# Adapter tail with its second products in high and low parts, and shares spread over partitions out of one SBUF row instead of a DRAM array

## The reference, cut to what matters

```python
# layer 0, after a convolution and causal attention (16 heads)
probs = jax.nn.softmax(tok @ gate_w.T, axis=-1)
topv, topi = jax.lax.top_k(probs, TOP_K)                     # 2 of 8 experts
topw = topv / (jnp.sum(topv, axis=-1, keepdims=True) + 1e-09)
combine = jnp.zeros((T, E), tok.dtype).at[jnp.arange(T)[:, None], topi].set(topw)
eo = jnp.einsum('eti,edi->etd', jax.nn.silu(eg) * eu, wd)    # inner width 176
moe_out = jnp.einsum('te,etd->td', combine, eo)
# layer 1: modulated attention and a GELU feed-forward, then
probs = jax.nn.softmax(x_flat @ Wr.T + br, axis=-1)
expert_idx, expert_weight = jnp.argmax(probs, axis=-1), jnp.max(probs, axis=-1)
h = jnp.einsum('nd,erd->ner', x_flat, A)                     # 8 adapters of rank 64
y = jnp.einsum('ner,eor->neo', h, B) * SCALING
out = take_along_axis(y, expert_idx) * expert_weight         # added to x
```

## Time and profile before

| what | us |
|---|---|
| median of 3 runs | 627.74 |
| lowest to highest | 626.38 to 632.41 |
| the profiled execution | 626.71 |
| its span in the profile | 624.6 |
| PE busy | 593.3 |
| DVE, ACT, POOL busy | 377.1, 341.1, 209.7 |

### The profile page before, as it was taken

One profiled execution on the slowest core, in us unless ns is written; L12 is line 12 of the kernel. 1 busy time (PEld: TensorE's weight loads), 2 busy tenths in 40 slices (PEclk: granted clock), 3 DMA queues, 4 the chain that ended last, 5 costly groups with the idle time before them and its releaser, 6 DMA issues.

```text
span 624.6 us, 13447 instructions
## 1 busy us (share of the span) xinstructions
PE 593.3 (95%) x5492; PEld 500.1 (80%) x5492; DVE 377.1 (60%) x668; ACT 341.1 (55%) x864; POOL 209.7 (34%) x222
## 2 busy tenths in 40 slices
PE   4789999999999989999998999999999998999996
PEld 2678888888888878888877878888788887788875
DVE  4877778877886567886745253262515376684553
ACT  0778568866785534453446453555444456556440
POOL 0672444354436523552434040131403025432000
PEclk9899999999999999999999999999999999999999
DMA  7770000000000148355001030112110001300023
GB/s 204 273 274 7 2 2 2 3 2 2 1 3 6 59 111 267 119 180 174 2 1 44 26 101 2 34 36 68 47 57 0 2 0 36 84 18 1 0 70 134
DMA packets 13676, 38.35 MB, mean 61 GB/s; under 512 B 2320, under 2 KB 3856, under 8 KB 13008
## 3 DMA queue, kind: packets, MB, share of 16 engines
q1 hardware_dynamic: 13376, 36.46, 17.9%
q10 hardware_dynamic: 240, 1.05, 0.7%
HBM read 36.39 MB, written 1.11 MB: 60 GB/s over the span
## 4 chain that ended last, share of the span: by engine, by line
PE 80%; DVE 8%; ACT 5%; DMA 3%; issue 2%; SPq 1%; POOL 1%; ACTq 0%; DVEq 0%
PE ps L1537 20%; PE ps L1538 18%; PE ps L1539 18%; PE ps L1655 8%; PE ps L1845 4%; PE ps L1614 3%; PE ps L1644 2%; PE ps L1632 2%; PE ps L1833 1%; DVE strm_lo L1369 1%; DMA work<-in_cols 1%; PE ps L2031 1%; ACT strm_hi L932 1%; PE ps L1693 1%; SPq L447 1%
## 5 line engine op out<-in xcount | busy, mean ns | idle before, releaser
L519 POOL TENSOR_TENSOR w_lo<-raw_w,w_hi 128x1024 fp32r<-128x1024 f32 x24 | 58.6, 2460 | 159.1 <-ACT w_hi L666 139.4
L1369 DVE SCALAR_TENSOR_TENSOR strm_lo<-ps,col,strm_hi 128x512 fp32r<-128x512 f32 x32 | 24.0, 750 | 104.3 <-ACT strm_hi L932 103.4
L1537 PE MATMUL ps<-w_hi,act_hi 128*128 128x512 f32 x160 | 64.6, 404 | 3.9 <-ACT junk L659 3.1
L917 ACT ACTIVATE work<-ps,col 128x512 f32<-128x512 f32 x64 | 43.9, 689 | 44.6 <-PE ps L1539 44.6
L1537 PE MATMUL ps<-act_hi,w_hi 128*128 128x512 f32 x160 | 63.5, 397 | 3.1 <-ACT work L917 1.9
L1539 PE MATMUL ps<-w_hi,act_lo 128*128 128x512 f32 x160 | 62.5, 391 | 0.0
L1538 PE MATMUL ps<-w_lo,act_hi 128*128 128x512 f32 x160 | 62.5, 390 | 0.0
L1539 PE MATMUL ps<-act_hi,w_lo 128*128 128x512 f32 x160 | 62.4, 390 | 0.0
L1538 PE MATMUL ps<-act_lo,w_hi 128*128 128x512 f32 x160 | 62.3, 390 | 0.0
L1655 PE MATMUL ps<-raw_w,xT 128*128 128x256 f32 x256 | 61.3, 380 | 0.0
L1655 PEld LDWEIGHTS ps<-raw_w,xT 128*128 128x128 f32 x256 | 46.3, 190 | 5.3
(11 more groups left out here) (202 smaller groups left out, 1435.0 us busy)
## 6 DMA issues: line engine op xcount, KB each, us to landing
raw_w<-in_w_attn SPq DMA_DIRECT2D x20, 512.0 KB, 3.6
raw_s<-in_w_moe SPq DMA_DIRECT2D x11, 384.0 KB, 5.1
work<-comb_dram SPq DMA_DIRECT2D x21, 128.0 KB, 2.9
raw_w<-in_w_qkv SPq DMA_DIRECT2D x4, 512.0 KB, 6.2
raw_w<-in_w_o SPq DMA_DIRECT2D x1, 2048.0 KB, 9.0
work<-comb_dram SPq DMA_DIRECT2D x8, 256.0 KB, 5.2
raw_s<-in_w_ffn SPq DMA_DIRECT2D x8, 256.0 KB, 2.7
bd<-in_w_ada SPq DMA_DIRECT2D x1, 1536.0 KB, 7.1
```

The source lines that it names most:

```text
L519: G.tensor_tensor(flat(w_lo[:, slot]), raw, flat(f32(w_hi[:, slot])), ALU.subtract).then_inc(s_piece_lo, 1)
L917: A(dst[:, h * BANK:(h + 1) * BANK], src, ACT.Identity, bias=c_(b, 4 * j + h)).then_inc(s_q1_copied, 1)
L1369: V.scalar_tensor_tensor(flat(strm_lo[:, n % SS]), ps[:, 4 + n % 2, :], c_("bv", 4 * UNITS[u][0] + h), flat(f32(strm_hi[:, n % SS])), ALU. ...
L1537: mm(dst, ah, bh, start=start and i == 0, stop=False, **flags)
```

## The change

Two things are changed.

The array in DRAM goes. spread reads the row of cmbT or selT in SBUF directly, n times, and SP no longer stores it and waits. The number of spreads, their sizes and their place in SP's order stay:

```diff
-            def spread(dst, layer, m, width, done_sem, s=slice(0, TOK)):
+            def spread(dst, rows, m, width, done_sem, s=slice(0, TOK)):
...
-                    sp.dma_start(dst[at:at + n, :], comb_dram[layer, e:e + 1, s].broadcast_to([n, s.stop - s.start])).then_inc(done_sem, 16)
+                    sp.dma_start(dst[at:at + n, :], rows[e:e + 1, s].unsqueeze(1).broadcast_to([1, n, s.stop - s.start])).then_inc(done_sem, 16)
...
                 sp.wait_ge(s_combT_ready, c + 1)
-                sp.dma_start(comb_dram[0, :, s], cmbT[0:NE, s]).then_inc(st_comb, 16)
-                sp.wait_ge(st_comb, 16 * (c + 1))
                 for m in range(SS):
-                    spread(cb[:, m, s], 0, m, INTER, (ld_cb, ld_cb_second)[c][m], s)
+                    spread(cb[:, m, s], cmbT, m, INTER, (ld_cb, ld_cb_second)[c][m], s)
...
                 sp.wait_ge(s_hm_ready, UNIT[m - SS, CHUNKS - 1] + 1)
-                spread(cb[:, m % SS, :], 0, m, INTER, ld_cb[m % SS])
+                spread(cb[:, m % SS, :], cmbT, m, INTER, ld_cb[m % SS])
...
                 sp.wait_ge(s_selT_ready, c + 1)
-                sp.dma_start(comb_dram[1, :, s], selT[0:NE, s]).then_inc(st_comb, 16)
-                sp.wait_ge(st_comb, 16 * (CHUNKS + c + 1))
                 for n in range(c * MR, (c + 1) * MR):
                     m = LORA[n][0]
-                    spread(cb1[:, m, s], 1, m, RANK, ld_cb1[n], s)
+                    spread(cb1[:, m, s], selT, m, RANK, ld_cb1[n], s)
```

The adapters' second products are made from high and low parts. ACT rounds the weight rows and hmk, POOL and DVE subtract for the low parts, and PE's three matmuls take the place of one in f32. The order of the tail on PE and ACT is changed, and DVE's four additions stand behind all multiplies:

```diff
+            for i, m in enumerate(ROWS):
+                pool.wait_ge(s_rows_hi, i + 1)
+                G.tensor_tensor(rows_lo[:, m, :], rows_of(m), f32(rows_hi[:, m, :]), ALU.subtract).then_inc(s_rows_lo, 1)
...
+                if n >= NF - 3:
+                    act.wait_ge(s_ffn_down, MM + 2)
+                    for m in (ROWS[0:2], ROWS[2:3], ROWS[3:4])[n - NF + 3]:
+                        A(rows_hi[:, m, :], rows_of(m), ACT.Copy).then_inc(s_rows_hi, 1)
+
+            def hmk_hi(n):
+                act.wait_ge(s_hmk32, n + 1)
+                act.wait_ge(s_lora_up, MR)
+                if n >= 2:
+                    act.wait_ge(s_hmk_used, n - 1)
+                A(act_hi[:, n % 2, 0:BANK], hmk[:, n % 3, :], ACT.Copy).then_inc(s_hmk_hi, 1)
+
             router_exp(0)
             take_ups(0, 2)
             x4_hi(1)
-            take_ups(2, MR)
+            take_ups(2, 3)
             take_selT(0)
             router_exp(1)
-            take_ups(MR, NL)
+            take_ups(3, 6)
             take_selT(1)
+            take_ups(6, 7)
+            hmk_hi(0)
+            take_ups(7, NL)
+            for n in range(1, NL):
+                hmk_hi(n)
...
+            def share_lo(n):
+                dve.wait_ge(s_hmk_hi, n + 1)
+                V.tensor_tensor(act_lo[:, n % 2, 0:BANK], hmk[:, n % 3, :], f32(act_hi[:, n % 2, 0:BANK]),
+                                ALU.subtract).then_inc(s_hmk_ready, 1)
+
+            share(0)
+            for n in range(1, NL):
+                share(n)
+                share_lo(n - 1)
+            share_lo(NL - 1)
+            for a in range(TILES // 2):
+                add_lora(a)
...
-                    last = mm(ps[:, bank, (t % 2) * D:(t % 2 + 1) * D], hmk[:, n % 3, t * P:(t + 1) * P], rows,
-                              start=(n % MR == 0 and t % 2 == 0), stop=(n % MR == MR - 1), skip_group_check=True)
+                    own = slice(t * P, (t + 1) * P)
+                    last = split_mm(ps[:, bank, (t % 2) * D:(t % 2 + 1) * D],
+                                    [(act_hi[:, n % 2, own], act_lo[:, n % 2, own], rows_hi[:, m, :], rows_lo[:, m, :])],
+                                    start=(n % MR == 0 and t % 2 == 0), stop=(n % MR == MR - 1), skip_group_check=True)
...
             for n in range(NL):
-                if n == 2:
+                if n == 3:
                     logits1(1)
-                if n == MR:
                     turn_sel(0)
+                if n == 6:
+                    turn_sel(1)
                 lora_up(n)
-            turn_sel(1)
             for n in range(MR):
                 lora_down(n)
```

More of the change, by code:

```diff
@@ L113, in build_program @@
         ps = ctx.enter_context(nc.psum_tensor("ps", [P, 8, BANK], F32))
-        comb_dram = nc.dram_tensor("comb_dram", [2, NE, TOK], F32, kind="Internal").ap()
         def c_(name, k=0, n=1):
@@ L219, in build_program @@
         ld_slice = [sem(f"ld_slice{i}") for i in range(SS)]
-        st_comb = sem("st_comb")
         ld_cb = [sem(f"ld_cb{i}") for i in range(SS)]
@@ L333, in build_program @@
         s_wsel = sem("wsel")
+        s_hmk32 = sem("hmk32")
+        s_hmk_hi = sem("hmk_hi")
         s_hmk_ready = sem("hmk_ready")
+        s_rows_hi = sem("rows_hi")
+        s_rows_lo = sem("rows_lo")
+        s_lora_sum = sem("lora_sum")
         block = ctx.enter_context(nc.Block())
@@ L382, in z2_at, with rows_of @@
             return hid[:, CT + t, :] if t < CT else z2[:, t, :]
+        rows_hi, rows_lo = (w[:, 2].rearrange("p a b -> p (a b)").rearrange("p (m n) -> p m n", m=MR) for w in (w_hi, w_lo))
+        ROWS = (0, MR - 1, 1, 2)
+        def rows_of(m):
+            return raw_t[:, 1, 2 * D:3 * D] if m == MR - 1 else raw_t[:, (MM + m) % SS, D:2 * D]
         LORA = [(m, c) for c in range(CHUNKS) for m in (0, 3, 1, 2)]
@@ L1504, in _, with add_lora, share @@
             router_pick(1)
[L1506 to L1512, removed]
-            for n, (m, c) in enumerate(LORA):
+            def add_lora(a):
+                if a % 2 == 0:
+                    dve.wait_ge(s_lora_sum, a // 2 + 1)
+                else:
+                    dve.wait_ge(s_hmk_used, MR * (a // 2 + 1))
+                t2 = slice(2 * a, 2 * a + 2)
+                V.tensor_tensor(xres[:, t2, :], ps[:, (a + 2) % 4, :].rearrange("p (b n) -> p b n", b=2),
+                                xres[:, t2, :], ALU.add).then_inc(s_y_ready, 1)
+            def share(n):
+                m, c = LORA[n]
                 dve.wait_ge(s_up_copied, n + 1)
@@ L1517, in _ @@
                 if n >= 3:
-                    dve.wait_ge(s_hmk_used, n - 2)
+                    dve.wait_ge(s_hmk_ready, n - 2)
                 V.tensor_tensor(hmk[:, n % 3, :], h1[:, n, :], cb1[:, m, c * BANK:(c + 1) * BANK],
-                                ALU.mult).then_inc(s_hmk_ready, 1)
-                if n == MR + 2:
-                    add_lora(0)
-            add_lora(1)
+                                ALU.mult).then_inc(s_hmk32, 1)
+            def share_lo(n):
[9 more added lines that the diff above has]
+                add_lora(a)
         @block.tensor
@@ L2026, in lora_down @@
                 pe.wait_ge(s_hmk_ready, n + 1)
-                rows = raw_t[:, 1, 2 * D:3 * D] if m == MR - 1 else raw_t[:, (MM + m) % SS, D:2 * D]
+                pe.wait_ge(s_rows_lo, ROWS.index(m) + 1)
                 for t in range(CT):
                     bank = (2 * c + t // 2 + 2) % 4
-                    last = mm(ps[:, bank, (t % 2) * D:(t % 2 + 1) * D], hmk[:, n % 3, t * P:(t + 1) * P], rows,
-                              start=(n % MR == 0 and t % 2 == 0), stop=(n % MR == MR - 1), skip_group_check=True)
+                    own = slice(t * P, (t + 1) * P)
+                    last = split_mm(ps[:, bank, (t % 2) * D:(t % 2 + 1) * D],
+                                    [(act_hi[:, n % 2, own], act_lo[:, n % 2, own], rows_hi[:, m, :], rows_lo[:, m, :])],
+                                    start=(n % MR == 0 and t % 2 == 0), stop=(n % MR == MR - 1), skip_group_check=True)
+                    if n % MR == MR - 1 and t == 1:
+                        last.then_inc(s_lora_sum, 1)
                 last.then_inc(s_hmk_used, 1)
             for n in range(NL):
-                if n == 2:
+                if n == 3:
                     logits1(1)
-                if n == MR:
                     turn_sel(0)
+                if n == 6:
+                    turn_sel(1)
                 lora_up(n)
-            turn_sel(1)
             for n in range(MR):
```

## The result

The changed kernel takes 797.88 us (median of 4 runs, 796.69 to 799.87) against 628.62 for the one before beside it (626.38 to 632.41): a ratio of 1.267, interval 1.261 to 1.273. The forecast was 834, with a range of 695 to 888. The direction and the cause were right; the loss is 169 us and not 207.

A forecast was written before the change was run, and what follows sets the result against it. PE was taken to bound the kernel, except for a last 25 us chained through DRAM round trips. The profiled 626.7 us plus 147 (expert stage) and 60 (tail) gave 833.7, forecast as 834 us, range 695 to 888.

The forecast's parts named there:

- The price, 27.3 GB/s for a block: All spreads: reading one SBUF row gets the rate of one block of four adjacent partitions, 27.3 GB/s.
- Rival A: All spreads: one-row reads go as fast as from DRAM, SP's issue stays the limit; 624 us, chance 0.20.
- rival B: All spreads: the source as a whole is limited to 51 GB/s; 699 us, chance 0.08 including speeds towards the forecast.
- C: All spreads: one DMA engine moves all, 26 GB/s, engines' share one sixteenth; chance within the forecast's 0.72.
- Step 1: Expert stage: shares read from one SBUF row land late, last at 439.5, and DVE's multiply waits; +147 us.
- 5.90 MB at 421 GB/s, 14.0 us: Expert stage: expert slices and attention pieces between the spreads in the first-in-first-out queue add 14.0 us.
- All engines wait behind DVE's multiply: Expert stage: nothing of the next stage can go ahead of DVE's multiply in the engines' orders.
- The 2 us for PE's clock: After the expert stage's wait: 2 us lost as PE's clock is granted at 0.74 when it runs again.
- Step 2: Adapter products: 96 matmuls of 256 columns replace 32 in f32, 11.5 us, 2.8 us gained on PE if fed.
- Step 3: Tail order: earlier turns and no store let the first spread go out at 597.8, 3.4 us earlier.
- Step 4: Tail transfers: adapter spreads from one SBUF row land late, end at 684.4 against 624.6; +60 us.
- 2.10 MB at 27.3 GB/s: Tail: the adapters' 16 spreads at one block's rate take 76.8 us.

The follow-up runs named there:

- e1: Changed kernel with the DRAM array, its stores and waits put back, split adapter products and new order kept; 629.17 us, ratio 0.999.
- e4: Changed kernel with each expert's row of shares on 16 partitions (e, e+8, ...), spreads reading 16 SBUF rows, not one; 626.67 us, ratio 0.995.
- e5: e4 with four places, not two, for the adapters' high and low parts, and chunk 0's additions before the last subtraction; 625.71 us, ratio 0.995.
- e3: Changed kernel with the tail's spreads issued tile 0, 1, 3, 2 in place of 0, 3, 1, 2; 809.04 us, ratio 1.285.
- e8: Kernel before with sixteen-row spreads out of SBUF and no DRAM array, its own tail with f32 adapter products kept; 630.54 us, ratio 1.001.

## Why the prediction came out as it did

**The price, 27.3 GB/s for a block: right.** It was taken from a row at full share and few partitions. The first half tiles run at 27.2, and the last four tiles, all in one block, land from 349.37 to 426.88: 2.10 MB in 77.5 us, 27.1. Rival A is out (e1 and e4 show what it would have been), rival B is out (27, not 51), and so is C: the share is 0.88 to 0.92, not 0.06.

**Step 1, +147, measured +131.9.** Of these, 2.2 us lie ahead of everything that the change touches: the first copy of shares starts at 214.59, before at 212.43. With that taken off, the last share, forecast for 439.5 and used at 426.96, came 14.7 us early. The term that failed is "5.90 MB at 421 GB/s, 14.0 us". The stage took about as long as if these loads were free: the first spread was issued at 215.18, and 0.75 us to the first byte and 5.77 MB at 27.3 make 427.2. But that this fits so well is partly luck, for the landings show a cost that stayed and a gain that I hadn't priced:

- The loads are free only in part. Four attention pieces stand behind the last half tile (landed 274.74); tile 3 landed at 297.44, 22.7 us later, where its 524 KB alone need 19.3. So these loads cost 3.4 us of the 5.0 I gave them. Between the spreads of the last four tiles stand 2.62 MB of loads, 6.2 us at 421 GB/s, and those 77.5 us are what the spreads alone need (77.1 at 27.2).
- Tiles 5 and 6 took 32.4 us and not 38.5 (317.01 to 349.37). There the spreads pass from experts 0 to 3 to experts 4 to 7, and two blocks are read side by side.

The stretch of 320 to 336 us, 60 GB/s at a share of 0.85, holds both: tile 5 from two blocks, and the slice that landed at 334.31. That engines which are done with their part of a spread go on to the load behind it, while the others still wait for the block, is my reading; no experiment tests it.

"All engines wait behind DVE's multiply" was wrong in part, too. DVE waited 77.6 us for shares and not over 100, and for part of the stage it was the expert weights that were late. Both stand in one queue, so the stage's length is the queue's all the same. The rest of the step held: 3 us of catching up were 3.4 (the last four multiplies take 9.13 us, before 12.54). The 2 us for PE's clock didn't come: from the last multiply to the last addition it took 288.9 us, before 288.75. Inside the stage and the tail the clock did fall, and matmuls took longer (the down products' first ones 366 ns in the mean, before 314), so PE counts 627.2 us busy and not the forecast 590.

**Step 2, PE's 2.8 us.** Right as a size, as e5 shows (11.8 us in place of 14.3), and right that waits would eat it here. It isn't free with quick transfers either: e1 gives it back to the round through ACT and DVE. Case A's sum, 2.7 us under before, is near e4, which is that case: 2.05 us by the tails.

**Step 3, 3.4 us earlier.** The first spread is issued 4.42 us after the last addition, before 8.15: 3.7.

**Step 4, +60, measured +38.7.** The term that failed is 2.10 MB at 27.3 GB/s. They took 55 us, from 730.2 (first bytes) to 785.2, 38 GB/s. LORA's order of tiles is 0, 3, 1, 2: experts 0 and 1, then 6 and 7, then 2 and 3, then 4 and 5. Neighbours in the queue lie in different blocks and run beside each other in part. I had priced each tile by one block and not asked what the next one reads. e3 took that away and lost 11 us.

So both misses have one root: I added up the transfers as if each had the queue to itself. Reads of different blocks run side by side in part, and loads to all partitions add little time of their own. The queue does hold back when they land, as the expert weights show.

## What to carry to other kernels

Before moving the source of a broadcast from DRAM to SBUF, count two things: how many limits of 27 GB/s the source's partitions reach (a block of four partitions and the one 32 on are one), and how many engines its outer dimension allows. Then ask what else stands in the same queue: it lands behind the slow transfer, and whoever needs it waits as well. Replicate the row by the engine that makes it (e8, with sixteen copies, is no slower than the kernel before) rather than reading one partition many times. An edit that shortens PE's work in a tail pays only when the transfers ahead and the buffers behind it are eased with it.

## What the runs showed of the hardware that I had not expected

A DMA issue can block the issuing engine. The spreads' line on SP, first before the change and then after it (ns for one issue: least, median, most; then us to landing):

```profile
L447 SPq DMA_DIRECT2D work<-comb_dram x44: 309/546/601, 214.5 to 612.9; - x44
...
DMA to landing us min/median/max: 2.5/3.0/9.8
```

```profile
L455 SPq DMA_DIRECT2D work<-work x44: 478/2140/18228, 215.2 to 773.2; - x44
...
DMA to landing us min/median/max: 7.0/15.0/55.9
```

One issue took 18.2 us, and the sixteen of the tail 48: SP stands at the spread and can't issue what is next. Loads behind the spreads are caught the same way (one expert slice took 18.3 us to issue, before 0.4 to 0.6). The DMA engines' share is no measure of work: 0.92 at 26 GB/s, and 0.26 at 99. And a kernel whose PE starves also pays in clock: TensorE's granted clock was 0.50 to 0.60 of the full 2.4 GHz, at or near its lower level of 1.2, in the stretches shown above in which PE stood still or had long pauses (283 to 296, 320 to 336 and 735 to 785 us), and 1.00 where it was fed.
